# A convolution stage with its variance as one fp32 product, its casts on ScalarE and its low halves on VectorE

## The chip, the cores and the metric

The kernel runs on one core of one Trainium2 chip. The metric is the device time of one execution in microseconds (us). Five engines with queues of their own work side by side: TensorE (PE in the profile), VectorE (DVE), ScalarE (ACT), GpSimd (POOL) and SyncE (SP), which only issues DMAs here. They meet through semaphores: an instruction adds to one when it is done, another engine waits until it has reached a value.

## The reference, cut to what matters

The reference is a block of two layers on an image tensor of 16 x 64 x 56 x 56: a gated shift convolution and a mixture of experts, then a binary-weight convolution and a second mixture of experts. The stage in question computes the third and the fourth step of this:

```python
x = x + _L0_conv_ref(_ln_c(x), ...)
t = t + _L0_ffn_ref(_ln_t(t), ...)
x = x + _L1_conv_ref(_ln_c(x), L1_conv_weights, L1_conv_real_scaling_factor)   # this stage
t = t + _L1_ffn_ref(_ln_t(t), ...)     # its inner _ln_t(t) is made in this stage

def _ln_c(v, eps=1e-06):
    m = jnp.mean(v, axis=1, keepdims=True)
    s = jnp.var(v, axis=1, keepdims=True)
    return (v - m) / jnp.sqrt(s + eps)
```

`_L1_conv_ref` is a 3 x 3 convolution of 64 to 64 channels with the signs of the weights, padded by one pixel, times a factor for each output channel. `_ln_t` is the same normalisation over the channels with eps 1e-5.

## The kernel before, in words

The image tensor stays in SBUF as X, 56 tiles of 128 partitions (64 channels of two images) by 448 elements (8 rows of 56 pixels). Seven tiles make one pair of images. The stages before the one in question normalise, gate, shift, and run the first mixture of experts; those after it compute the routing of the second mixture (L1100 to L1203) and run it (L1208 to L1433). They read what this stage stores: XN4 (the normalised tile) and SD4 (its high and low half).

The stage runs from L871 to L1075. Each tile n is normalised (ln3), split into a high half in float32r and a low half (the rest), both written into padded images pad_hi and pad_lo; the convolution of tile n is 9 shifts times two halves, 18 products of 128 x 448 in float32r that accumulate in PSUM; X is updated with it; the new X is normalised again (ln4), split, and stored. ln3 runs three tiles ahead of the convolution (LEAD = 3), ln4 two tiles behind it.

One normalisation (class Norm, L120 to L224) is a chain through the engines:
- pe_centre (L158): PE multiplies the tile by the matrix CEN in fp32, which gives the tile minus its channel mean in PSUM. An fp32 product appears as two matmuls, each with a weight load.
- act_square: ACT squares it. With split set it does so twice, once rounded to float32r (sq_hi, L164) and once in fp32 (sq, L166). pool_square_lo (L173): POOL subtracts the one from the other.
- pe_var: with split set two float32r products with AVGR, of sq_hi (L182) and sq_lo (L183), into one PSUM tile; without it one fp32 product of sq with AVG (L187).
- act_r (L198) and act_rr (L204): ACT takes the reciprocal square root r and squares it.
- dve_newton: DVE computes q (L209) and g (L212), one Newton step. dve_scale (L219): DVE multiplies the centred tile by g.

ln3 and ln4 have two PSUM buffers for the centred tile and one for the variance, and one SBUF buffer for everything else (nx = 2, nv = 1, depth = 1). The other stages use Norm without split.

The order within a step n is written out by hand for each engine:
- PE: centre3(n+3), conv(n), var4(n-2), centre4(n-1), var3(n+3). The convolution waits until pad_lo of tile n+1 is written.
- ACT: squares of ln3(n+3), seed4(n-2) (r and rr), squares of ln4(n-1), seed3(n+3).
- DVE: norm3(n+2) (q, g, xn, and the cast into pad_hi, L1009), X(n) (L1028), norm4(n-2) (q, g, xn with a sum, and the cast into hi, L1017).
- POOL: low squares of ln3(n+3) (L173), lo3(n+2) (pad_lo, L1051), low squares of ln4(n-1), lo4(n-2) (lo, L1056).
- SP: stores of XN4 and of the two halves for tile n (L916, L919, L921).

The first 14 steps and the last 14 are unrolled, the 28 between run as two passes of a hardware loop with tile numbers in registers. The order of PE ahead of the first convolution is centre3(0), centre3(1), var3(0), centre3(2), var3(1), var3(2); POOL makes every low half there as well.

Of the kernel before, what the change touches and what calls it, by code (L numbers as in the profile page):

```python
# [16 lines left out]
F32 = mybir.dt.float32  # L17
F32R = mybir.dt.float32r
# [5 lines left out]
P = 128  # L24
# [22 lines left out]
def build(nc, A, out):  # L47
# [178 lines left out]
    with top:  # L226
# [644 lines left out]
        with ExitStack() as ctx:  # L871
# [3 lines left out]
            AVGR = sbuf(ctx, "average_r", [P, P], F32R)  # L875
# [11 lines left out]
            average_ready = sem(ctx, "p5_average")  # L887
# [9 lines left out]
            def every_step(engine, step):  # L897


                for i in units(engine, NP // 2 - 1):  # L900
                    for m in range(V):
                        step(V * i + m, m)
                for m in range(V):
                    step(NT - V + m, m)

            with nc.Block() as block:
                @block.sync
                def _(sp):
                    sp.dma_start(cwraw[:], A["conv_w"]).then_inc(consts, 16)
                    for a in range(2):  # L910
                        sp.dma_start(sf[C * a:C * a + C, :], A["factor"]).then_inc(consts, 16)

                    def store(n, m):

                        sp.wait_ge(ln4.normed, n + 1)
                        sp.dma_start(XN4[bass.ds(n, 1)].rearrange("o p w -> (o p) w"), xn4[:, m % 2])\  # L916
                            .then_inc(stored[m % 2], 16)
                        sp.wait_ge(hi_done, n + 1)
                        sp.dma_start(split_rows(SD4, n, 0), hi[:, m % 2].bitcast(F32)).then_inc(stored[m % 2], 16)  # L919
                        sp.wait_ge(lo_done, n + 1)  # L920
                        sp.dma_start(split_rows(SD4, n, 1), lo[:, m % 2].bitcast(F32)).then_inc(stored[m % 2], 16)  # L921

                    every_step(sp, store)
                    for b in range(2):
                        sp.wait_ge(stored[b], 48 * NT // 2)

                @block.tensor
                def _(pe):
                    pe.wait_ge(average_ready, 1)

                    def conv(n, m):
                        pair, k = divmod(m, KT)
                        pe.wait_ge(pad_lo_done, n + 1 + min(1, KT - 1 - k))
                        wait(pe, x3_done, n - 1)
                        o = rows(cps[:, m % 2, 0:TW])
# [7 lines left out]
                    def centre4(n, m):  # L943
                        pe.wait_ge(x3_done, n + 1)
                        ln4.pe_centre(pe, n, m, tile(X, n))

                    def step(n, m):
                        if exists(n + LEAD):
                            ln3.pe_centre(pe, n + LEAD, m + LEAD, tile(X, n + LEAD))
                        conv(n, m)  # L950
                        if exists(n - 2):
                            ln4.pe_var(pe, n - 2, m)
                        if exists(n - 1):
                            centre4(n - 1, m + 1)
                        if exists(n + LEAD):
                            ln3.pe_var(pe, n + LEAD, m + LEAD)

                    for k in range(LEAD):
                        ln3.pe_centre(pe, k, k, tile(X, k))
                        if k >= 1:  # L960
                            ln3.pe_var(pe, k - 1, k - 1)
                    ln3.pe_var(pe, LEAD - 1, LEAD - 1)
                    pe.wait_ge(signed, 1)
                    pe.wait_ge(zeroed, 8)
                    every_step(pe, step)
                    ln4.pe_var(pe, NT - 2, 0)
                    centre4(NT - 1, 1)
                    ln4.pe_var(pe, NT - 1, 1)

                @block.scalar  # L970
                def _(act):
                    act.activation(AVGR[:], AVG[:], ACT.Copy).then_inc(average_ready, 1)

                    def step(n, m):
                        if exists(n + LEAD):
                            ln3.act_square(act, n + LEAD, m + LEAD)
                        if exists(n - 2):
                            ln4.act_seed(act, n - 2, m, 1)
                        if exists(n - 1):
                            ln4.act_square(act, n - 1, m + 1)  # L980
                        if exists(n + LEAD):
                            ln3.act_seed(act, n + LEAD, m + LEAD, 0)

                    for k in range(LEAD):
                        ln3.act_square(act, k, k)
                        if k >= 1:
                            ln3.act_seed(act, k - 1, k - 1, 0)
                    ln3.act_seed(act, LEAD - 1, LEAD - 1, 0)
                    act.wait_ge(consts, 48)
                    act.activation(cw[:], cwraw[:], ACT.Sign).then_inc(signed, 1)  # L990
                    every_step(act, step)
                    ln4.act_seed(act, NT - 2, 0, 1)
                    ln4.act_square(act, NT - 1, 1)
                    ln4.act_seed(act, NT - 1, 1, 1)

                @block.vector
                def _(dve):
                    for border in borders(pad_hi):
                        dve.memset(border, 0.0).then_inc(zeroed, 1)

                    def norm3(n, m):

                        pair, k = divmod(m, KT)
                        wait(dve, pad_lo_done, n - 1)
                        ln3.dve_norm(dve, n, m, EPS_C, xn3[:, m % 2])
                        dve.wait_ge(ln3.normed, n + 1)
                        if k == 0:
                            wait(dve, conv_done, n - KT)
                        dve.tensor_copy(pad_hi[:, pair, ROWS * k + 1:ROWS * k + 1 + ROWS, 1:WW + 1], rows(xn3[:, m % 2]))\  # L1009
                            .then_inc(pad_hi_done, 1)  # L1010

                    def norm4(n, m):

                        wait(dve, stored[m % 2], past_stores(n, m))
                        ln4.dve_norm(dve, n, m, EPS_T, xn4[:, m % 2], accum=MSUM[:, bass.ds(n, 1)])
                        dve.wait_ge(ln4.normed, n + 1)
                        dve.tensor_copy(hi[:, m % 2], xn4[:, m % 2]).then_inc(hi_done, 1)  # L1017

                    def past_stores(n, m):

                        return 24 * (n - m % 2)

                    def step(n, m):
                        if exists(n - 1) and exists(n + LEAD - 1):
                            norm3(n + LEAD - 1, (m + LEAD - 1) % V)
                        dve.wait_ge(conv_done, n + 1)
                        x = tile(X, n)
                        dve.scalar_tensor_tensor(out=x, in0=cps[:, m % 2, 0:TW], scalar=sf[:, 0:1], in1=x,  # L1028
                                                 op0=ALU.mult, op1=ALU.add).then_inc(x3_done, 1)
                        if exists(n - 2):  # L1030
                            norm4(n - 2, m)

                    for k in range(LEAD):
                        norm3(k, k)
                    dve.wait_ge(consts, 48)
                    every_step(dve, step)
                    norm4(NT - 2, 0)
                    norm4(NT - 1, 1)

                @block.gpsimd  # L1040
                def _(pool):
                    for border in borders(pad_lo):
                        pool.memset(border, 0.0).then_inc(zeroed, 1)  # L1043

                    def lo3(n, m):
                        pair, k = divmod(m, KT)
                        inside = (slice(None), pair, slice(ROWS * k + 1, ROWS * k + 1 + ROWS), slice(1, WW + 1))
                        pool.wait_ge(pad_hi_done, n + 1)
                        if k == 0:
                            wait(pool, conv_done, n - KT)  # L1050
                        pool.tensor_tensor(pad_lo[inside], rows(xn3[:, m % 2]), pad_hi[inside].bitcast(F32), ALU.subtract)\  # L1051
                            .then_inc(pad_lo_done, 1)

                    def lo4(n, m):
                        pool.wait_ge(hi_done, n + 1)
                        pool.tensor_tensor(lo[:, m % 2], xn4[:, m % 2], hi[:, m % 2].bitcast(F32), ALU.subtract)\  # L1056
                            .then_inc(lo_done, 1)

                    def step(n, m):
                        if exists(n + LEAD):  # L1060
                            ln3.pool_square_lo(pool, n + LEAD, m + LEAD)
                        if exists(n - 1) and exists(n + LEAD - 1):
                            lo3(n + LEAD - 1, (m + LEAD - 1) % V)
# [441 lines left out]
```

## Time and profile before

| | us |
|---|---|
| median of 3 runs | 2896.38 |
| lowest and highest of the 3 | 2887.58 and 2897.5 |
| the profiled execution | 2888.95 |
| its span in the trace | 2887.0 |
| from the first product of the stage to its last GpSimd instruction | 2082.0 to 2469.0 |
| mean granted clock of PE over the span | 0.964 of full |
| PE busy over the span | 2641.3 (91%) |
| DVE busy over the span | 1493.1 (52%) |
| ACT busy over the span | 1582.3 (55%) |
| POOL busy over the span | 509.4 (18%) |

The profiled execution lies 7.4 us under the median: two of the three runs stand at 2896 to 2898 and one at 2888. Busy time over the span mixes eight stages. In what follows the time between the starts of two instructions is called their pitch. It differs from the duration that a row gives: a DVE or ACT instruction that depends on the one before starts a little after its end, an independent one up to 0.1 us before its end, and matmuls overlap further.

### The profile page before, as it was taken

The numbers are of one execution on the slowest core, as the hardware profiler recorded it, in microseconds if no ns is written. First come the engines' busy times: TensorE is split into PE (matmuls) and PEld (weight loads), VectorE is DVE, ScalarE is ACT, GpSimd is POOL, SyncE is SP. The second block draws the span as 40 slices with busy tenths as digits, with TensorE's granted clock in tenths as the row PEclk, the third lists the DMA queues.
The fourth block names the chain that finished last, engine by engine and source line by source line (L and its number), as shares of the span: only waits on it lengthen the run. The fifth ranks groups of instructions, "written<-read, shape, count | busy, mean of one in ns | idle before, by whom it ended". The sixth has DMA issues, their size and how long they took to land. (4 is left out here: it accounts for less than half of the span.)

```text
span 2887.0 us, 42401 instructions
## 1 busy us (share of the span) xinstructions
PE 2641.3 (91%) x12188; PEld 1488.0 (52%) x12188; DVE 1493.1 (52%) x2823; ACT 1582.3 (55%) x2305; POOL 509.4 (18%) x408
## 2 busy tenths in 40 slices
PE   8976786999999999999999999999889999298897
PEld 5642444555555555555555555555467777133343
DVE  6632888344444444444444444443369998245545
ACT  5630565555555555555555555555556665167666
POOL 3320775000000000000000000000068887100000
PEclk9988898999999999999999999999989999599999
DMA  4467676434243333424333342433113232475552
GB/s 133 131 144 161 176 201 179 107 76 96 64 97 75 86 87 74 96 64 97 77 83 90 72 96 65 96 78 83 41 58 115 106 115 106 116 181 150 163 158 81
DMA packets 168940, 308.47 MB, mean 107 GB/s; under 512 B 50626, under 2 KB 161058, under 8 KB 161570
## 3 DMA queue, kind: packets, MB, share of 16 engines
q1 hardware_dynamic: 168866, 307.60, 41.7%
q8 instruction: 32, 0.52, 0.1%
q14 instruction: 42, 0.34, 0.0%
HBM read 210.12 MB, written 97.39 MB: 107 GB/s over the span
## 5 line engine op out<-in xcount | busy, mean ns | idle before, releaser
L781 ACT ACTIVATE hidden<-hidden_psum,b 128x896 f32<-128x896 f32 x896 | 853.9, 1004 | 706.3 <-PE hidden_psum L730 706.3
L847 DVE SCALAR_TENSOR_TENSOR weighted<-y_psum,b,w_bc 128x448 f32<-128x448 f32 x448 | 306.4, 684 | 923.6 <-PE y_psum L744 909.8
L744 PE MATMUL y_psum<-hidden,w 128*64 128x448 f32 x3584 | 773.2, 552 | 2.1 <-DVE weighted L847 2.1
L729 PE MATMUL hidden_psum<-tokens,w1hi 128*128 128x448 f32 x1792 | 705.9, 394 | 14.0 <-DMA ident<-in_ident 11.2
L730 PE MATMUL hidden_psum<-tokens,w1lo 128*128 128x448 f32 x1792 | 660.5, 369 | 0.0
L729 PEld LDWEIGHTS hidden_psum<-tokens,w1hi 128*128 128x128 f32 x1792 | 336.7, 188 | 332.9 <-ACT hidden L781 294.2
L744 PEld LDWEIGHTS y_psum<-hidden,w 128*64 128x64 f32 x3584 | 217.7, 136 | 350.4 <-issue 244.0
L730 PEld LDWEIGHTS hidden_psum<-tokens,w1lo 128*128 128x128 f32 x1792 | 338.0, 189 | 24.3
L198 ACT ACTIVATE ln_r<-ln_var,eps 128x448 f32<-128x448 f32 x280 | 177.4, 634 | 235.9 <-PE ln_var L183 135.3
L158 PE MATMUL ln_xc<-X,centre 128*128 (+1 forms) x448 | 226.1, 588 | 74.7 <-DVE X L608 55.8
L1043 POOL MEMSET pad_lo<- 128x116 f32 (+1 forms) x4 | 0.8, 266 | 1591.6 <-POOLq L665 1591.6
L855 DVE TENSOR_TENSOR X<-X,weighted 128x448 f32 (+1 forms) x448 | 278.1, 621 | 2.9
L212 DVE SCALAR_TENSOR_TENSOR ln_g<-ln_q,ln_r 128x448 f32<-128x448 f32 x280 | 234.7, 838 | 9.7
L209 DVE SCALAR_TENSOR_TENSOR ln_q<-ln_var,ln_rr 128x448 f32<-128x448 f32 x280 | 172.9, 617 | 97.4 <-ACT ln_rr L204 96.0
L939 PE MATMUL conv_psum<-pad_hi,conv_sign 128*128 128x448 f32 x504 | 197.7, 392 | 1.5 <-POOL pad_lo L1051 1.4
L939 PE MATMUL conv_psum<-pad_lo,conv_sign 128*128 128x448 f32 x504 | 188.5, 374 | 0.0
L187 PE MATMUL ln_var<-ln_sq,average 128*128 128x448 f32 x336 | 163.2, 572 | 17.7 <-DVE ln_q L209 17.4
L1378 ACT ACTIVATE hidden<-hidden_psum,b1sel 128x448 f32<-128x448 f32 x224 | 130.3, 630 | 76.0 <-PE hidden_psum L1325 75.5
L166 ACT ACTIVATE ln_sq<-ln_xc 128x448 f32<-128x448 f32 x224 | 120.2, 537 | 93.9 <-PE ln_xc L158 93.8
L173 POOL TENSOR_TENSOR ln_sq_lo<-ln_sq,ln_sq_hi 128x448 fp32r<-128x448 f32 x112 | 160.9, 1437 | 45.1 <-ACT ln_sq L166 45.1
L204 ACT ACTIVATE ln_rr<-ln_r 128x448 f32<-128x448 f32 x280 | 161.7, 578 | 8.9
L219 DVE SCALAR_TENSOR_TENSOR xn<-ln_xc,ln_g 128x448 f32<-128x448 f32 x224 | 139.9, 625 | 40.0 <-DMA scr_xlr<-xn 20.1
(128 smaller groups left out, 2442.5 us busy)
## 6 DMA issues: line engine op xcount, KB each, us to landing
w_bc<-scr_wtok SPq DMA_DIRECT2D x112, 896.0 KB, 10.6
tokens<-scr_split SPq DMA_DIRECT2D x224, 224.0 KB, 3.7
scr_split<-hi SPq DMA_DIRECT2D x112, 224.0 KB, 2.0
scr_split<-lo SPq DMA_DIRECT2D x112, 224.0 KB, 1.9
scr_xn<-xn SPq DMA_DIRECT2D x56, 224.0 KB, 2.0
tokens_plus_y<-scr_xn SPq DMA_DIRECT2D x56, 224.0 KB, 2.8
out<-out_tile SPq DMA_DIRECT2D x56, 224.0 KB, 2.0
X<-in_x SPq DMA_DIRECT2D x6, 1792.0 KB, 7.6
```

What stands on the lines that cost most here:

```text
L158: pe.matmul(self.xc[:, b, 0:TW], CEN[:], x, start=True, stop=True).then_inc(self.centred, 1)
L187: pe.matmul(self.var[:, self.at(m, self.nv), 0:TW], AVG[:], self.sq[:, self.at(m, self.depth)], start=True, stop=True).then_inc(self.var_r ...
L198: act.activation(self.r[:, b], self.var[:, self.at(m, self.nv), 0:TW], ACT.Abs_reciprocal_sqrt, bias=EPS[:, eps_col:eps_col + 1]).then_inc ...
L209: dve.scalar_tensor_tensor(out=self.q[:, b], in0=self.var[:, self.at(m, self.nv), 0:TW], scalar=eps, in1=self.rr[:, b], op0=ALU.add, op1=A ...
L212: dve.scalar_tensor_tensor(out=self.g[:, b], in0=self.q[:, b], scalar=-3.0, in1=self.r[:, b], op0=ALU.add, op1=ALU.mult).then_inc(self.g_d ...
L729: pe.matmul(o, w1hi[:, s * P:(s + 1) * P], S[:, b, a, :], start=True, stop=False)
L730: mm = pe.matmul(o, w1lo[:, s * P:(s + 1) * P], S[:, b, a, :], start=False, stop=True)
L744: mm = pe.matmul(yp[C * a:C * a + C, e % 2, 0:TW], w2[:, e, c, :], hs[:, s % (2 * CH0), a, :], start=(c == 0), stop=(c == CH0 - 1))
L781: act.activation(hs[:, k % (2 * CH0)], hp[:, k % 2, :, 0:TW], ACT.Gelu, bias=b1[:, e, c:c + 1])\
L847: dve.scalar_tensor_tensor(out=pr[:, e % 2], in0=yp[:, e % 2, 0:TW], scalar=b2[:, e:e + 1], in1=WB[:, b, e, :], op0=ALU.add, op1=ALU.mult) ...
L855: dve.tensor_tensor(x, x, pr[:, e % 2], ALU.add).then_inc(summed, 1)
L939: mm = pe.matmul(o, cw[:, t9, :], src[:, pair, ROWS * k + dy:ROWS * k + dy + ROWS, dx:dx + WW], start=(t9 == 0 and part == 0), stop=(t9 == ...
```

## The change

In the convolution stage alone:
- ln3 and ln4 are made without split: one square on ACT (L166), one fp32 product on PE (L187) instead of two float32r ones, no low squares. AVGR goes, and the wait for it.
- The casts into pad_hi and hi move from DVE to ACT (high3, high4, ACT Copy).
- The subtractions into pad_lo and lo move from POOL to DVE (low3, low4). POOL keeps only the zeroing of pad_lo's borders.
- The steps are all unrolled, without registers.
- Orders: PE runs centre3(n+3) behind conv(n) instead of ahead of it, and centre3, var3 tile by tile at the start. ACT runs high3(n+2), square3(n+3), seed4(n-2), square4(n-1), seed3(n+3), high4(n-2). DVE runs norm3(n+2), low3(n+2), X(n), norm4(n-2), low4(n-2).

```diff
-            ln3 = Norm(ctx, "ln3", 2, 1, depth=1, split=AVGR)
-            ln4 = Norm(ctx, "ln4", 2, 1, depth=1, split=AVGR)
+            ln3 = Norm(ctx, "ln3", 2, 1, depth=1)
+            ln4 = Norm(ctx, "ln4", 2, 1, depth=1)
...
                 @block.tensor
...
+                    for n in range(LEAD):
+                        centre3(n)
+                        ln3.pe_var(pe, n, n)
                     pe.wait_ge(signed, 1)
                     pe.wait_ge(zeroed, 8)
...
+                    for n in range(NT):
+                        conv(n)
+                        if n + LEAD < NT:
+                            centre3(n + LEAD)
+                        if n >= 2:
+                            ln4.pe_var(pe, n - 2, n - 2)
+                        if n >= 1:
+                            centre4(n - 1)
+                        if n + LEAD < NT:
+                            ln3.pe_var(pe, n + LEAD, n + LEAD)
...
                 @block.scalar
...
+                    def high3(n):
+                        act.wait_ge(ln3.normed, n + 1)
+                        if n % KT == 0 and n >= V:
+                            act.wait_ge(conv_done, n - KT)
+                        act.activation(inside(pad_hi, n), rows(xn3[:, n % 2]), ACT.Copy).then_inc(pad_hi_done, 1)
+
+                    def high4(n):
+                        act.wait_ge(ln4.normed, n + 1)
+                        if n >= 2:
+                            act.wait_ge(stored[n % 2], 48 * (n // 2))
+                        act.activation(hi[:, n % 2], xn4[:, n % 2], ACT.Copy).then_inc(hi_done, 1)
+
+                    for n in range(LEAD):
+                        ln3.act_square(act, n, n)
+                        ln3.act_seed(act, n, n, 0)
+                        if n < LEAD - 1:
+                            high3(n)
                     act.wait_ge(consts, 48)
                     act.activation(cw[:], cwraw[:], ACT.Sign).then_inc(signed, 1)
...
+                    for n in range(NT + 2):
+                        if n + LEAD - 1 < NT:
+                            high3(n + LEAD - 1)
+                        if n + LEAD < NT:
+                            ln3.act_square(act, n + LEAD, n + LEAD)
+                        if 2 <= n:
+                            ln4.act_seed(act, n - 2, n - 2, 1)
+                        if 1 <= n <= NT:
+                            ln4.act_square(act, n - 1, n - 1)
+                        if n + LEAD < NT:
+                            ln3.act_seed(act, n + LEAD, n + LEAD, 0)
+                        if 2 <= n:
+                            high4(n - 2)
...
                 @block.vector
...
+                    def low3(n):
+                        dve.wait_ge(pad_hi_done, n + 1)
+                        if n % KT == 0 and n >= V:
+                            dve.wait_ge(conv_done, n - KT)
+                        dve.tensor_tensor(inside(pad_lo, n), rows(xn3[:, n % 2]), inside(pad_hi, n).bitcast(F32), ALU.subtract)\
+                            .then_inc(pad_lo_done, 1)
...
+                    def low4(n):
+                        dve.wait_ge(hi_done, n + 1)
+                        dve.tensor_tensor(lo[:, n % 2], xn4[:, n % 2], hi[:, n % 2].bitcast(F32), ALU.subtract)\
+                            .then_inc(lo_done, 1)
```

## Rows read from the trace of the kernel before

**Rows 1.** Windows of the stage: busy of PE, PEld, DVE, ACT, POOL; clock; DMA.

```profile
2113.00:2454.00 341.00, 339.54 (x1414) 260.10 (x1413) 310.95 (x532) 214.69 (x424) 268.69 (x212) 1.00 0.29 106
...
2082.00:2107.00 25.00, 7.67 (x15) 3.21 (x15) 6.89 (x15) 8.79 (x14) 5.80 (x7) 0.60 0.08 24
```

**Rows 2.** Timeline of one step, PE: start, duration, instruction, idle before it.

```profile
2251.47 0.37 PE L939 MATMUL conv_psum<-pad_lo,conv_sign 128*128 128x448 f32 x1
...
2254.82 0.37 PE L939 MATMUL conv_psum<-pad_lo,conv_sign 128*128 128x448 f32 x1
...
2255.43 0.92 PE L158 MATMUL ln_xc<-X,centre 128*128 x2
...
2257.30 0.19 PEld L939 LDWEIGHTS conv_psum<-pad_hi,conv_sign 128*128 128x128 f32 x1 [0.51 <-POOL pad_lo L1051]
```

**Rows 3.** Timeline of the last stage: weight loads of unsplit variance products.

```profile
2728.47 0.19 PEld L187 LDWEIGHTS ln_var<-ln_sq,average 128*128 128x128 f32 x1 [0.19 <-issue]
...
2729.22 0.19 PEld L187 LDWEIGHTS ln_var<-ln_sq,average 128*128 128x128 f32 x1 [0.19 <-issue]
```

**Rows 4.** Timeline of the stage: one step of DVE, and the rr that releases it.

```profile
2256.98 0.62 DVE L209 SCALAR_TENSOR_TENSOR ln_q<-ln_var,ln_rr 128x448 f32<-128x448 f32 x1 [0.29 <-ACT ln_rr L204]
...
2260.10 1.14 DVE L212 SCALAR_TENSOR_TENSOR ln_g<-ln_q,ln_r 128x448 f32<-128x448 f32 x1
...
2262.45 0.58 ACT L204 ACTIVATE ln_rr<-ln_r 128x448 f32<-128x448 f32 x1
...
2263.13 0.62 DVE L209 SCALAR_TENSOR_TENSOR ln_q<-ln_var,ln_rr 128x448 f32<-128x448 f32 x1
```

**Rows 5.** Timeline of the second normalisation's stage: DVE to ACT to POOL.

```profile
487.54 0.62 DVE L219 SCALAR_TENSOR_TENSOR xn<-ln_xc,ln_g 128x448 f32<-128x448 f32 x1
...
488.20 0.58 ACT L581 ACTIVATE hi<-xn 128x448 fp32r<-128x448 f32 x1 [2.48 <-DVE xn L219]
...
488.85 1.13 POOL L543 TENSOR_TENSOR lo<-xn,hi 128x448 fp32r<-128x448 f32 x1 [1.93 <-ACT hi L581]
```

**Rows 6.** The same stage: ACT.

```profile
305.56 0.53 ACT L166 ACTIVATE ln_sq<-ln_xc 128x448 f32<-128x448 f32 x1
305.98 0.63 ACT L198 ACTIVATE ln_r<-ln_var,eps 128x448 f32<-128x448 f32 x1
306.64 0.58 ACT L204 ACTIVATE ln_rr<-ln_r 128x448 f32<-128x448 f32 x1
...
310.41 0.56 ACT L581 ACTIVATE hi<-xn 128x448 fp32r<-128x448 f32 x1
310.88 0.52 ACT L166 ACTIVATE ln_sq<-ln_xc 128x448 f32<-128x448 f32 x1
```

**Rows 7.** The same stage: DVE, a two-input subtraction's like.

```profile
305.98 0.62 DVE L608 TENSOR_TENSOR X<-X,shifted 128x448 f32<-128x448 f32 x1
306.52 0.62 DVE L209 SCALAR_TENSOR_TENSOR ln_q<-ln_var,ln_rr 128x448 f32<-128x448 f32 x1
307.17 0.62 DVE L212 SCALAR_TENSOR_TENSOR ln_g<-ln_q,ln_r 128x448 f32<-128x448 f32 x1
307.83 0.62 DVE L219 SCALAR_TENSOR_TENSOR xn<-ln_xc,ln_g 128x448 f32<-128x448 f32 x1
```

**Rows 8.** Timeline, the 56 updates of X: tiles 0, 34 and 55.

```profile
2112.99 0.68 DVE L1028 SCALAR_TENSOR_TENSOR X<-conv_psum,factor,X 128x448 f32<-128x448 f32 x1 [5.76 <-PE conv_psum L939]
...
2325.09 0.67 DVE L1028 SCALAR_TENSOR_TENSOR X<-conv_psum,factor,X 128x448 f32 x1
...
2454.33 0.68 DVE L1028 SCALAR_TENSOR_TENSOR X<-conv_psum,factor,X 128x448 f32<-128x448 f32 x1 [0.61 <-PE conv_psum L939]
```

**Rows 9.** Timeline: a table load, the first convolution product, the last of POOL.

```profile
2087.14 1.28 ACT L198 ACT_TABLE_LOAD   x1
...
2106.84 1.25 PE L939 MATMUL conv_psum<-pad_hi,conv_sign 128*128 128x448 f32 x1
...
2467.89 1.13 POOL L1056 TENSOR_TENSOR lo<-xn,hi 128x448 fp32r<-128x448 f32 x1 [3.54 <-DVE hi L1017]
```

More of the change, by code:

```diff
@@ L874, in build @@
             sf = sbuf(ctx, "factor", [P, 1])
-            AVGR = sbuf(ctx, "average_r", [P, P], F32R)
             pad_hi = sbuf(ctx, "pad_hi", [P, 2, HH + 2, PADW], F32R)
@@ L895, in borders, with inside @@
                 return p[:, :, 0, :], p[:, :, HH + 1, :], p[:, :, 1:HH + 1, 0], p[:, :, 1:HH + 1, WW + 1]
[L897 to L904, printed above, removed]
+            def inside(pad, n):
+                pair, k = divmod(n % V, KT)
+                return pad[:, pair, ROWS * k + 1:ROWS * k + 1 + ROWS, 1:WW + 1]
             with nc.Block() as block:
@@ L911, in _, with conv @@
                         sp.dma_start(sf[C * a:C * a + C, :], A["factor"]).then_inc(consts, 16)
-                    def store(n, m):
+                    for n in range(NT):
+                        b = n % 2
                         sp.wait_ge(ln4.normed, n + 1)
-                        sp.dma_start(XN4[bass.ds(n, 1)].rearrange("o p w -> (o p) w"), xn4[:, m % 2])\
-                            .then_inc(stored[m % 2], 16)
+                        sp.dma_start(XN4[n], xn4[:, b]).then_inc(stored[b], 16)
                         sp.wait_ge(hi_done, n + 1)
-                        sp.dma_start(split_rows(SD4, n, 0), hi[:, m % 2].bitcast(F32)).then_inc(stored[m % 2], 16)
+                        sp.dma_start(SD4[n, 0], hi[:, b].bitcast(F32)).then_inc(stored[b], 16)
                         sp.wait_ge(lo_done, n + 1)
-                        sp.dma_start(split_rows(SD4, n, 1), lo[:, m % 2].bitcast(F32)).then_inc(stored[m % 2], 16)
-                    every_step(sp, store)
+                        sp.dma_start(SD4[n, 1], lo[:, b].bitcast(F32)).then_inc(stored[b], 16)
                     for b in range(2):
                         sp.wait_ge(stored[b], 48 * NT // 2)
+                @block.gpsimd
+                def _(pool):
+                    for border in borders(pad_lo):
+                        pool.memset(border, 0.0).then_inc(zeroed, 1)
                 @block.tensor
                 def _(pe):
-                    pe.wait_ge(average_ready, 1)
-                    def conv(n, m):
-                        pair, k = divmod(m, KT)
+                    def conv(n):
+                        pair, k = divmod(n % V, KT)
                         pe.wait_ge(pad_lo_done, n + 1 + min(1, KT - 1 - k))
-                        wait(pe, x3_done, n - 1)
-                        o = rows(cps[:, m % 2, 0:TW])
+                        if n >= 2:
+                            pe.wait_ge(x3_done, n - 1)
+                        o = rows(cps[:, n % 2, 0:TW])
                         for t9 in range(9):
@@ L941, in conv, with centre3, centre4 @@
                         mm.then_inc(conv_done, 1)
-                    def centre4(n, m):
+                    def centre3(n):
+                        ln3.pe_centre(pe, n, n, X[:, n])
+                    def centre4(n):
                         pe.wait_ge(x3_done, n + 1)
[L945 to L962, printed above, removed]
+                        ln4.pe_centre(pe, n, n, X[:, n])
+                    for n in range(LEAD):
+                        centre3(n)
+                        ln3.pe_var(pe, n, n)
                     pe.wait_ge(signed, 1)
                     pe.wait_ge(zeroed, 8)
-                    every_step(pe, step)
@@ L966, in _ @@
-                    ln4.pe_var(pe, NT - 2, 0)
-                    centre4(NT - 1, 1)
-                    ln4.pe_var(pe, NT - 1, 1)
+                    for n in range(NT):
+                        conv(n)
[7 more added lines that the diff above has]
+                            ln3.pe_var(pe, n + LEAD, n + LEAD)
@@ L970, in _ @@
+                    ln4.pe_var(pe, NT - 2, NT - 2)
+                    centre4(NT - 1)
+                    ln4.pe_var(pe, NT - 1, NT - 1)
                 @block.scalar
                 def _(act):
[L972 to L988, printed above, removed]
+                    def high3(n):
[3 more added lines that the diff above has]
+                        act.activation(inside(pad_hi, n), rows(xn3[:, n % 2]), ACT.Copy).then_inc(pad_hi_done, 1)
@@ new lines, in high4 @@
+                    def high4(n):
+                        act.wait_ge(ln4.normed, n + 1)
+                        if n >= 2:
+                            act.wait_ge(stored[n % 2], 48 * (n // 2))
[5 more added lines that the diff above has]
+                            high3(n)
@@ L996, in _, with norm3 @@
                 @block.vector
                 def _(dve):
+                    def norm3(n):
+                        if n >= 2:
+                            dve.wait_ge(pad_lo_done, n - 1)
+                        ln3.dve_norm(dve, n, n, EPS_C, xn3[:, n % 2])
+                    def low3(n):
[4 more added lines that the diff above has]
+                            .then_inc(pad_lo_done, 1)
@@ L998, in _, with norm4 @@
+                    def norm4(n):
+                        if n >= 2:
+                            dve.wait_ge(stored[n % 2], 48 * (n // 2))
+                        ln4.dve_norm(dve, n, n, EPS_T, xn4[:, n % 2], accum=MSUM[:, n:n + 1])
+                    def low4(n):
+                        dve.wait_ge(hi_done, n + 1)
+                        dve.tensor_tensor(lo[:, n % 2], xn4[:, n % 2], hi[:, n % 2].bitcast(F32), ALU.subtract)\
+                            .then_inc(lo_done, 1)
                     for border in borders(pad_hi):
@@ L999, in _ @@
                         dve.memset(border, 0.0).then_inc(zeroed, 1)
[L1001 to L1031, printed above, removed]
@@ L1033, in _ @@
-                    for k in range(LEAD):
-                        norm3(k, k)
-                    dve.wait_ge(consts, 48)
[L1036 to L1063, printed above, removed]
-                        if exists(n - 1):
-                            ln4.pool_square_lo(pool, n - 1, m + 1)
-                        if exists(n - 2):
-                            lo4(n - 2, m)
-                    for k in range(LEAD):
-                        ln3.pool_square_lo(pool, k, k)
-                        lo3(k, k)
-                    every_step(pool, step)
-                    ln4.pool_square_lo(pool, NT - 1, 1)
-                    lo4(NT - 2, 0)
-                    lo4(NT - 1, 1)
@@ new lines, in _ @@
+                    for n in range(LEAD - 1):
+                        norm3(n)
+                        low3(n)
+                    dve.wait_ge(consts, 48)
+                    for n in range(NT + 2):
+                        if n + LEAD - 1 < NT:
+                            norm3(n + LEAD - 1)
+                        if n + LEAD - 1 < NT:
+                            low3(n + LEAD - 1)
+                        if n < NT:
+                            dve.wait_ge(conv_done, n + 1)
+                            dve.scalar_tensor_tensor(out=X[:, n], in0=cps[:, n % 2, 0:TW], scalar=sf[:, 0:1], in1=X[:, n],
+                                                     op0=ALU.mult, op1=ALU.add).then_inc(x3_done, 1)
+                        if n >= 2:
+                            norm4(n - 2)
+                            low4(n - 2)
```

5 lines of the change are left out of this document (removed).

## The prediction

> **What bounds the kernel now.** I read the windows first, then the timeline of one step, then the rows of X(n). Only one stage changes, so only its share of the span matters. In its steady part PE is busy 339.5 of 341 us at full clock and DVE 311 of 341, ACT 215 and POOL 269 [rows 1]. PE's busy time counts overlapping matmuls, so pitches have to confirm it. The 56 updates of X run from 2112.99 to 2454.33: 55 steps of 6.206 us [rows 8].
>
> PE in a step: 16 pitches of convolution products take 3.35 us, 0.209 each, so 18 take 3.77. From the last of them to the centring behind the variance pair are 0.61, so the pair costs 0.40 [rows 2]. An fp32 product is two matmuls: three weight loads of the unsplit variance lie 0.375 apart (2728.47, one left out between, 2729.22), so one product costs 0.75 [rows 3]. A step has 3.77 + 2 x 0.40 + 2 x 0.75 = 6.07 us of array work in 6.206. PE then waits for pad_lo from POOL for a moment: its weight loader stood 0.51 us, of which the array feels about 0.1, since the centring still drains [rows 2].
>
> DVE in the same step goes from q3 to the next q3 in 6.15 us, nearly without a gap, and one of its two g instructions takes 1.14 instead of 0.62 us [rows 4, 7]. So both engines are full today: work taken from one gains nothing alone, and work or a wait added to either lengthens the step.
>
> **The change part by part, PE.** Each of the two variance pairs becomes one fp32 product: 0.40 to 0.75. The step's array work is 3.77 + 4 x 0.75 = 6.77 us. Nothing hides it: 0.56 over the step of today. This is a floor for the new step.
>
> **DVE and ACT.** DVE loses two casts, gains two subtractions of two SBUF operands, and is rid of POOL's company. But each subtraction now waits for a cast that ACT can only begin when DVE's xn is done: DVE stands still for a round trip twice a step. DVE to ACT: from the start of xn to the start of the copy 0.66 us; from there to the start of the waiting subtraction 0.65 [rows 5] (the waiter there is POOL; DVE behind ACT's rr waits 0.68 from rr's start, whose duration is the same 0.58 [rows 4], so the price for each trip lies between 0.65 and 0.68 and I take 0.65).
>
> ACT is in order too. high3(n+2) stands ahead of square3 and seed4, so DVE's q4 can't start until ACT went through all of them. Pitches on ACT: copy 0.47, square 0.42, r 0.66 [rows 6], and rr to q 0.68 [rows 4]. On DVE: q 0.65, g 0.66, and subtraction to an independent q 0.54 (the row is an addition of two SBUF tiles in the same shape, 0.62 us long) [rows 7].
>
> I follow one step from q3 at 0: xn3 at 1.31; high3 on ACT at 1.97; square3 at 2.44; r4 at 2.86; rr4 at 3.52; q4 at 4.20. DVE's own path to q4 is shorter: low3 at 1.97 + 0.65 = 2.62, X at 3.16, free at about 3.87, so q4 is held 0.3 us by ACT. Then xn4 at 5.51; high4 on ACT at 6.17 (ACT is free from about 5.7: square4 at 4.0, r3 at 4.4, rr3 at 5.1); low4 at 6.82; the next q3 at 7.36. Step 7.36 us.
>
> Does PE hold any of this back? Its 6.77 leave 0.59 of slack, which falls in front of var3(n+3): that needs square3, done at about 3.0. conv(n+1) then runs from 3.8 to 7.5, centre3 to 8.3, var4 to 9.05. In the next step's count these are 0.9 and 1.7, ahead of 2.44 and 2.86. low3(n+2) is written at 3.25, ahead of conv(n+1). centre3 behind the convolution instead of ahead of it costs nothing by this. The stores of a buffer have two steps to land. So the loop through DVE and ACT sets the step, at +1.15 us over 6.206.
>
> **Start of the stage.** Before, POOL stands in each of the three first chains, and the first convolution starts at 2106.84 [rows 9]. After: with the first centring at 2081.7 and the square at 2082.75, r waits for a table load of 1.28 us [rows 9], and xn3(0) ends at 2087.9. Each further tile is one chain of copy, square, variance, r, rr, q, g, xn without overlap: about 0.55 + 0.55 + 1.9 + 0.67 + 0.68 + 1.93 = 6.3 us, where 1.9 is the fp32 product at half clock (the granted clock is 0.60 over this stretch [rows 1], and PE idles more now). xn3(1) ends at 2094.3; square, variance, r, rr of tile 2 and the signs take 5.3: the first convolution at 2099.6, 7.3 us earlier than today, its end as much earlier.
>
> **Steps and tail.** X(0) at 2105.7. The first three steps are irregular (PE late, then a lag of 1.05 us once): X(3) at 2126.8. Then 50 steps of 7.36: X(53) at 2494.8. The last two steps lack ln3 and take 4.2 and 3.8: X(55) at 2502.8. From X(0) to X(55) these are 397.1 us against 341.3 [rows 8]: +55.8. Behind X(55) three rounds of q, g, xn, copy and subtraction (3.3 each) take 10.2 us to the end of the last subtraction, against 14.7 today (2454.33 to 2467.89 + 1.13 [rows 8, 9]): -4.5.
>
> Sum: -7.3 + 55.8 - 4.5 = +44.0 us.
>
> **Unrolling.** Costed at nothing. The loop holds tiles 14 to 41. The first 34 steps, over half of them in it, take 6.24 us each, the last 21, a third of them in it, 6.15 [rows 8]: what an unrolled step may save is of the order of 0.1. With DVE waiting, a branch would be hidden as well. Bounds: 0.1 us x 28 = 3 us gained, 3 us lost to code loading.
>
> **POOL and the shared port.** The row shows a g of 1.14 us where POOL computes beside it, against 0.62 elsewhere [rows 4, 7]: 0.52 a step that comes back. It is in my sum already, as every DVE pitch is of undisturbed rows. The Trainium skill (SBUF - State Buffer, "Who interferes with whom") says that VectorE's instructions with two SBUF inputs contend for a port pair with GpSimd instructions that read SBUF; the trace agrees by that row. By that rule alone, with a VectorE that bounds the stage, leaving GpSimd out would make the stage faster: that is the third rival.
>
> **Against the times.** On the profiled execution's 2888.95 the sum gives 2933. The runs before fall into a group near 2897 and one near 2888; on the median the same sum gives 2940. I forecast 2937, between.
>
> **Rivals.** (1) PE alone sets the step, at 6.77. It would be so if the two round trips were hidden. Against it: one buffer depth and the order written out leave DVE nothing else to do between xn and low. 50 x 0.59 = 30 less: +14, about 2907, at the edge of what can be told from no change.
>
> (2) The clock. PE is full-clocked at 99.6% busy; after, it works 6.77 of 7.36 us (92%) with a short stop in each step. If the granted clock fell to 0.9 in the mean, its work would be 7.5 us and the step with it: +7 us more. At 0.8 it would be 8.5: +56 more, about 2993. Against it: over the whole span, PE is 91% busy and the mean clock 0.96.
>
> (3) The other side: the stage gets faster, because DVE is what binds. DVE's instructions without any wait are 5.7 us a step (2 x 1.31 + 2 x 0.66 + 2 x 0.54 + 0.7), 0.4 less than today's 6.15. With the fp32 product at no more than the pair's 0.40, and the copies done before DVE looks for them, the step would be 6.07: -7.5 over 55 steps, with start and tail -19, 2872 on my middle. It decides from a step under 6.42 us on, where start and tail outweigh the rest. Against it: 0.75 for the product, in every unsplit row of the other stages.
>
> (4) The round trips cost more than priced, or PE and DVE hold each other up in turn: steps of 7.6 to 7.8, +12 to +22 more, up to 2959.
>
> **How the numbers follow.** Chances: the forecast 0.70, PE alone 0.12, the clock 0.04, faster 0.03, dearer trips 0.11. The forecast's own range is 2925 to 2949: 0.03 us for each round trip and 0.05 for each of the other unknown pitches make the step 7.3 to 7.5 (-3 to +7), unrolling 3 each way, and the two levels of the runs 4 each way. It holds 0.70, so the range takes in what lies next: down to the PE-bound case at 2907, up to most of case 4 at 2957. A measurement of this kernel tells about 0.5% (14 us) from no change: under 2882 faster, to 2911 the same. Faster 0.03; the same 0.11 (nearly all of the first rival); slower 0.86.
>
> **What would show it.** X(n) 7.3 to 7.5 us apart; the first convolution product near 2099.6; the longest waits of the stage those of DVE's two subtractions for ACT's copies, about 0.6 us before each, and of q4 for rr of some 0.3; no g over 0.7 us; PE standing before var3 for the square (about 0.6 a step) and the stage's clock still 1.00. If PE has no gap and steps are 6.8, the first rival holds. If q4 has no wait, ACT's order is not what I think. Stages before and after should not move; if they do, the prediction is wrong for a reason that I don't have.

## The result, and the profile after

| | before | changed |
|---|---|---|
| median of 4 runs each, us | 2894.8 | 2936.1 |
| lowest and highest | 2887.6 to 2897.5 | 2935.3 to 2939.1 |
| profiled execution | 2888.95 | 2939.14 |
| its span | 2887.0 | 2937.1 |

The changed kernel is slower by some 1.5%: the ratio is 1.0149, 95% interval 1.0128 to 1.0169, 41.3 us between the medians. Between the two profiled executions it is 50.2, because the one of before lies 5.9 under its median and the one of after 3.0 above.

The stage alone, from its first centring to the end of its last subtraction, took 387.0 us and takes 435.2: +48.2. The stages ahead of it differ by 2.2 us, those behind by 0.3. The first lies within what the start of the stage moves between kernels that differ only inside it: from 2081.9 us to 2087.2 in the eleven traces.

The updates of X in the changed kernel, from a timeline of VectorE (start, duration, instruction, idle before it; L1035 is L1028 of before). They answer [rows 8].

```profile
2107.53 0.68 DVE L1035 SCALAR_TENSOR_TENSOR X<-conv_psum,factor,X 128x448 f32<-128x448 f32 x1 [3.78 <-PE conv_psum L933]
...
2253.95 0.68 DVE L1035 SCALAR_TENSOR_TENSOR X<-conv_psum,factor,X 128x448 f32<-128x448 f32 x1
...
2261.31 0.68 DVE L1035 SCALAR_TENSOR_TENSOR X<-conv_psum,factor,X 128x448 f32<-128x448 f32 x1
...
2506.51 0.68 DVE L1035 SCALAR_TENSOR_TENSOR X<-conv_psum,factor,X 128x448 f32<-128x448 f32 x1
```

A step is 7.35 to 7.36 us in all but a few of the 55, against 6.206, which is the mean over all 55 of before, the irregular three at either end among them; the 49 between take 6.27. In what follows q3, xn3 are instructions of ln3, q4, xn4 of ln4, high is ScalarE's copy and low VectorE's subtraction. One step in the changed kernel, the whole loop through VectorE and ScalarE, from its timeline:

```profile
2250.83 0.62 DVE L209 SCALAR_TENSOR_TENSOR ln_q<-ln_var,ln_rr 128x448 f32<-128x448 f32 x1
...
2252.14 0.63 DVE L219 SCALAR_TENSOR_TENSOR xn<-ln_xc,ln_g 128x448 f32<-128x448 f32 x1
...
2252.80 0.58 ACT L969 ACTIVATE pad_hi<-xn 128x448 fp32r<-128x448 f32 x1 [2.55 <-DVE xn L219]
2253.28 0.53 ACT L166 ACTIVATE ln_sq<-ln_xc 128x448 f32<-128x448 f32 x1
2253.41 0.63 DVE L1009 TENSOR_TENSOR pad_lo<-xn,pad_hi 128x448 fp32r<-128x448 f32 x1 [0.64 <-ACT pad_hi L969]
2253.71 0.63 ACT L198 ACTIVATE ln_r<-ln_var,eps 128x448 f32<-128x448 f32 x1
...
2253.86 1.02 PE L187 MATMUL ln_var<-ln_sq,average 128*128 128x448 f32 x2 [0.29 <-ACT ln_sq L166]
...
2254.37 0.58 ACT L204 ACTIVATE ln_rr<-ln_r 128x448 f32<-128x448 f32 x1
...
2255.05 0.62 DVE L209 SCALAR_TENSOR_TENSOR ln_q<-ln_var,ln_rr 128x448 f32<-128x448 f32 x1 [0.41 <-ACT ln_rr L204]
...
2256.36 0.62 DVE L219 SCALAR_TENSOR_TENSOR xn<-ln_xc,ln_g 128x448 f32<-128x448 f32 x1
...
2257.03 0.58 ACT L975 ACTIVATE hi<-xn 128x448 fp32r<-128x448 f32 x1 [0.52 <-DVE xn L219]
...
2257.64 0.62 DVE L1019 TENSOR_TENSOR lo<-xn,hi 128x448 fp32r<-128x448 f32 x1 [0.65 <-ACT hi L975]
2258.18 0.62 DVE L209 SCALAR_TENSOR_TENSOR ln_q<-ln_var,ln_rr 128x448 f32<-128x448 f32 x1
```

Counted from q3 at 2250.83: xn3 1.31, high3 1.97, square 2.45, r4 2.88, rr4 3.54, q4 4.22, xn4 5.53, high4 6.20, low4 6.81, next q3 7.35. VectorE stands still three times, 0.64 and 0.65 for the copies and 0.41 for rr. None of ScalarE's squares waits for a centring, so PE's new order, which no run takes alone, isn't on this loop.

The waits of the stage's steady part, 2150 to 2450 us (engine, line, what it waited for: us in total, times, longest):

```profile
ACT pad_hi L969 <- DVE xn L219: 104.3, 41, 2.5
PEld ln_var L187 <- ACT ln_sq L166: 42.1, 41, 1.4
DVE lo L1019 <- ACT hi L975: 26.5, 41, 0.6
DVE pad_lo L1009 <- ACT pad_hi L969: 26.4, 41, 0.6
ACT hi L975 <- DVE xn L219: 21.6, 41, 0.9
DVE ln_q L209 <- ACT ln_rr L204: 17.3, 41, 0.8
...
PE ln_var L187 <- ACT ln_sq L166: 12.5, 41, 0.7
```

The top line is ScalarE waiting for work, which costs nothing. VectorE's three add up to 70.2 us in 41 steps, 1.71 each. PE stands too (0.3 a step by the last line, 1.0 by its weight loader's): neither engine is full, in a stage where PE was busy 339.5 of 341 us before and VectorE went through its step nearly without a gap [rows 1, 4]. The window of the steady part, columns as in [rows 1]:

```profile
2150.00:2400.00 250.00, 239.96 (x885) 164.10 (x884) 187.48 (x340) 143.70 (x273) 0.00 (x0) 1.00 0.26 94
```

### The profile page after: what moved, and what is told of

The parts are those of the page before. It is cut to its first block and busy times, and to the rows that moved or that the text cites. A ratio compares the mean times of both kernels' runs of the same rounds, so it can differ in the third digit from the quotient of the medians.

```text
span 2937.1 us, 41684 instructions
## 1 busy us (share of the span) xinstructions
PE 2690.2 (92%) x12188; PEld 1493.8 (51%) x12188; DVE 1477.6 (50%) x2823; ACT 1593.8 (54%) x2304; POOL 227.0 (8%) x184
## 5 line engine op out<-in xcount | busy, mean ns | idle before, releaser
L187 PE MATMUL ln_var<-ln_sq,average 128*128 128x448 f32 x560 | 275.9, 577 | 42.5 <-ACT ln_sq L166 21.9
L158 PE MATMUL ln_xc<-X,centre 128*128 128x448 f32 (+1 forms) x448 | 226.0, 588 | 62.9 <-DVE X L608 52.3
L212 DVE SCALAR_TENSOR_TENSOR ln_g<-ln_q,ln_r 128x448 f32<-128x448 f32 x280 | 208.4, 744 | 9.6
L933 PE MATMUL conv_psum<-pad_hi,conv_sign 128*128 128x448 f32 x504 | 207.9, 412 | 3.7 <-ACT conv_sign L983 2.4
L187 PEld LDWEIGHTS ln_var<-ln_sq,average 128*128 128x128 f32 x560 | 98.2, 194 | 154.9 <-ACT ln_sq L166 95.1
L166 ACT ACTIVATE ln_sq<-ln_xc 128x448 f32<-128x448 f32 x224 | 119.4, 533 | 102.7 <-PE ln_xc L158 102.6
L158 PEld LDWEIGHTS ln_xc<-X,centre 128*128 128x128 f32 x448 | 80.1, 197 | 139.3 <-issue 120.9
```

The costliest lines, as they stand in the source:

```text
L158: pe.matmul(self.xc[:, b, 0:TW], CEN[:], x, start=True, stop=True).then_inc(self.centred, 1)
L187: pe.matmul(self.var[:, self.at(m, self.nv), 0:TW], AVG[:], self.sq[:, self.at(m, self.depth)], start=True, stop=True).then_inc(self.var_r ...
L212: dve.scalar_tensor_tensor(out=self.g[:, b], in0=self.q[:, b], scalar=-3.0, in1=self.r[:, b], op0=ALU.add, op1=ALU.mult).then_inc(self.g_d ...
L933: mm = pe.matmul(o, cw[:, t9, :], src[:, pair, ROWS * k + dy:ROWS * k + dy + ROWS, dx:dx + WW], start=(t9 == 0 and part == 0), stop=(t9 == ...
```

## The experiments

Theory A is the prediction's: in each step VectorE and ScalarE hand work to and fro on one chain, which sets the step at 7.36 us. Its main rival B: the fp32 product makes TensorE's work longer, and that is what the step shows. "Stage" is measured as above; a median's difference holds the noise of whole runs, some 3 us.

| kernel | median | ratio to before, 95% interval | median step | stage |
|---|---|---|---|---|
| before | 2894.8 | | 6.21 | 387.0 |
| changed | 2936.1 | 1.0128 to 1.0169 | 7.35 | 435.2 |
| variance alone | 2907.5 | 1.0030 to 1.0064 | 6.79 | 406.0 |
| moves alone | 2970.0 | 1.0255 to 1.0296 | 7.79 | 465.7 |
| round trips hidden | 2907.8 | 1.0029 to 1.0062 | 6.79 | 405.7 |
| one rounded product | 2934.3 | 1.0127 to 1.0160 | 7.35 | 432.9 |
| one more copy | 2962.5 | 1.0225 to 1.0259 | 7.82 | 460.0 |
| one more copy, trips hidden | 2908.0 | 1.0034 to 1.0068 | 6.79 | 406.9 |
| seed ahead of the square | 2975.1 | 1.0265 to 1.0300 | 8.07 | 471.7 |
| before, unrolled | 2890.8 | 0.9985 to 1.0005 | 6.22 | 387.5 |
| best | 2847.7 | 0.9829 to 0.9861 | 5.69 | 345.7 |

Each ratio is to runs of the kernel before on the same chip, whose medians were 2891.8 to 2894.8. Differences to the changed kernel are between medians from different chips.

**Take the waits away.** VectorE is given other work while ScalarE copies:

```diff
                             norm3(n + LEAD - 1)
+                        if n >= 3:
+                            low4(n - 3)
...
                             norm4(n - 2)
-                            low4(n - 2)
```

> The changed kernel, with one order altered: VectorE runs low4(n-3) between xn3(n+2) and low3(n+2) instead of low4(n-2) right behind xn4(n-2), so that both casts on ScalarE run while VectorE has other work. Theory A (the loop through VectorE and ScalarE with two round trips sets the step of 7.36 us): VectorE's loop falls to about 6.2, TensorE's array work of 6.77 becomes the bound, steps of 6.8, 28 to 32 us less than the changed kernel: about 2906. Rival B (the dearer fp32 product on TensorE is what lengthened the step, the round trips lie beside it): steps stay at 7.3 to 7.4, 0 to 5 us less.

The step is 6.79 and the median 28.3 us under the changed kernel. Rival B is out for the part between 6.79 and 7.36. The window shows the other bound:

```profile
2150.00:2400.00 250.00, 250.00 (x958) 180.48 (x957) 199.55 (x369) 163.62 (x295) 0.00 (x0) 1.00 0.28 103
```

PE without a gap, at the 6.77 that its array work was counted to.

**Take the dearer product away.** Norm's square is written as float32r, and the variance is one float32r product of it:

```diff
-            self.sq = sbuf(ctx, tag + "_sq", [P, depth, TW])
+            self.sq = sbuf(ctx, tag + "_sq", [P, depth, TW], F32R if rounded else F32)
...
-            pe.matmul(self.var[...], AVG[:], self.sq[...],
+            pe.matmul(self.var[...], (self.rounded or AVG)[:], self.sq[...],
```

> The changed kernel, but the squares of ln3 and ln4 are rounded to float32r and the variance is one float32r product of them, 0.20 us instead of 0.75 (this leaves out the squares' low halves). TensorE's array work falls from 6.77 to 5.67 us a step. Theory A: steps stay at 7.36, as TensorE had slack anyway; only the three chains at the start, the lag in the third step and the tail gain, 3 to 7 us together: about 2931. Rival B: steps fall by 0.6 to 1.1, 30 to 60 us less than the changed kernel.

The step doesn't move, 7.35, though PE had 1.1 us a step less to do; the stage is 2.3 us shorter, from its start (1.1) and its steps and tail, less than the 3 to 7 expected. The waits of 2150 to 2400 show where PE's spare time goes, 1.4 us a step:

```profile
PEld ln_var L188 <- ACT ln_sq L167: 70.8, 34, 2.1
PE ln_var L188 <- ACT ln_sq L167: 46.3, 34, 1.4
```

With the experiment before it this settles which loop holds the changed kernel: shortening PE's work by 1.1 gives nothing, hiding VectorE's waits gives 0.57.

**Make the chain longer, in both.** A copy of xn3 into a spare tile, ahead of the one into pad_hi:

```diff
+                        act.activation(spare[:], xn3[:, n % 2], ACT.Copy)
                         act.activation(inside(pad_hi, n), ..., ACT.Copy).then_inc(pad_hi_done, 1)
```

> The changed kernel, with one more copy of xn3 on ScalarE, into a spare tile, ahead of the copy into pad_hi. Theory A (the copy lies on the loop through VectorE and ScalarE that sets the step): the copy's pitch of 0.47 us goes in full into each step, 7.83 us, over 54 steps 25 us more than the changed kernel: about 2961. Rival B (TensorE sets the step): no change, since ScalarE is busy 58% of the stage and TensorE has all it needs.

> The same extra copy, in the kernel whose round trips are hidden (low4 between xn3 and low3, 2907.8 us). There TensorE sets the step with 6.79, and the loop through VectorE and ScalarE needs about 6.2. Theory A: 6.2 + 0.47 = 6.67 stays under 6.79, so 0 to 3 us more, about 2909. If the copy costs 20 us here too, the loop still sets the step in the kernel with hidden trips, and TensorE's bound is not what held it at 6.79.

7.82 a step and 26.4 us more in the one, 6.79 and 0.2 us more in the other. The same instruction costs its full pitch (0.47) where it lies on the chain and nothing where TensorE binds.

**ScalarE's order.** The prediction had q4 held 0.3 us behind square3. Moving the seed up looks like the cure:

```diff
+                        if 2 <= n:
+                            ln4.act_seed(act, n - 2, n - 2, 1)
                         if n + LEAD < NT:
                             ln3.act_square(act, n + LEAD, n + LEAD)
-                        if 2 <= n:
-                            ln4.act_seed(act, n - 2, n - 2, 1)
```

> The changed kernel, with ScalarE running seed4(n-2) ahead of the square of ln3(n+3) (high3, seed4, square3, ...). Theory A followed through all engines: now TensorE's var3(n+3) waits for a square that stands behind seed4, which itself waits for var4: conv 3.77 + centre 0.75 + var4 0.75 + 0.17 + r 0.66 + rr 0.48 + square 0.54 + 0.05 + var3 0.75 = 7.92 us a step, 26 to 30 us more than the changed kernel: about 2964. Rival D (the only thing that counts on ScalarE is that q4 is held by 0.3 us behind the square): steps of 7.0 to 7.1, 12 to 18 us less.

It costs 39 us. The rival is out and the direction was right, the size was not: 8.07 a step instead of 7.92. Its timeline:

```profile
2300.00 1.02 PE L187 MATMUL ln_var<-ln_sq,average 128*128 128x448 f32 x2 [1.01 <-ACT ln_sq L166]
...
2304.66 0.92 PE L158 MATMUL ln_xc<-X,centre 128*128 128x448 f32 x2
...
2305.42 0.91 PE L187 MATMUL ln_var<-ln_sq,average 128*128 128x448 f32 x2
...
2306.37 0.63 ACT L198 ACTIVATE ln_r<-ln_var,eps 128x448 f32<-128x448 f32 x1 [0.47 <-PE ln_var L187]
...
2307.04 0.58 ACT L204 ACTIVATE ln_rr<-ln_r 128x448 f32<-128x448 f32 x1
2307.52 0.96 ACT L166 ACTIVATE ln_sq<-ln_xc 128x448 f32<-128x448 f32 x2
...
2308.10 0.30 PEld L187 LDWEIGHTS ln_var<-ln_sq,average 128*128 128x128 f32 x2 [1.73 <-ACT ln_sq L166]
```

From one var3 (2300.00) over the convolution to centre3 are 4.66 us, where 0.75 + 3.77 = 4.52 were counted: the product that restarts PE behind a wait takes 1.02 us, the next 0.91. That restart is most of the 0.15 that was missing. The chain is the one that was written down: var4, r, rr, square, var3.

**The parts alone.** The kernel before with the unsplit variance and nothing else (no low squares on GpSimd), and the changed kernel with the split variance put back:

```diff
-            ln3 = Norm(ctx, "ln3", 2, 1, depth=1, split=AVGR)
+            ln3 = Norm(ctx, "ln3", 2, 1, depth=1)
...
-                            ln3.pool_square_lo(pool, n + LEAD, m + LEAD)
```

> The kernel before with the variance alone changed: one fp32 product of unsplit squares, no low squares on GpSimd; casts stay on VectorE, low halves on GpSimd, the loop stays. Theory A: VectorE's own loop is 6.1 or less, TensorE binds with 6.77 of array work, steps of 6.8 to 6.85: +33 us over 55 steps, the start about 3 us shorter without GpSimd in its chains: +27 to +33 against the kernel before. Rival E (the kernel before was bound by VectorE and GpSimd, not by TensorE, and gains by the rest from the low squares): within 10 us of the kernel before.

> The changed kernel with the variance as in the kernel before: split squares, low squares on GpSimd, two float32r products. Only the casts (on ScalarE), the low halves (on VectorE), the orders and the unrolling are changed. Theory A: the same loop with one more square on ScalarE (0.43 us) between high3 and seed4 gives 7.8 us a step; GpSimd's low squares now lie beside g again and may lengthen it by up to 0.5: 7.8 to 8.3, over 53 steps 23 to 50 more than the changed kernel, 2960 to 2986, although TensorE's array work is back at 6.07 us. Rival B (TensorE's dearer product is what costs): back near the kernel before, under 2910.

The variance alone gives 6.79 a step, as counted, and 14.2 us in the medians, 18.9 in the stage. That is less than expected: the steps come to +27.3 us and not 33, since the first and the last few are shorter than the rest; the start is 5.6 us shorter, not 3; and the tail, which I had not counted, 2.7. The moves alone give 7.79, at the low end of the expectation, and are the dearest of the three: +78.7 in the stage. So the parts don't add up: +18.9 and +78.7 alone, +48.2 together. Two loops run through the stage and the longer one counts; the unsplit variance takes one square off the chain that the moves create, and its pitch of 0.43 is the whole of 7.79 less 7.36. Its own price on PE vanishes below that chain. GpSimd's low squares are not on it: PE stands 1.4 us a step for them (45.2 in 32 times, 2150 to 2400), as it has that slack, and g was not lengthened either, which the expectation allowed for (0.633 us in the mean).

**Unrolling.**

```diff
-                for i in units(engine, NP // 2 - 1):
-                    for m in range(V):
-                        step(V * i + m, m)
-                for m in range(V):
-                    step(NT - V + m, m)
+                for n in range(NT):
+                    step(n, n % V)
```

> The kernel before with its stage fully unrolled and nothing else changed. Prediction: VectorE and TensorE fill the step, branches lie beside them, so within 3 us of the kernel before either way. Rival F (the loop's branches and register work cost on the path): 6 us or more less. If code loading costs, 3 us or more above.

No difference: the stage 387.5 against 387.0, the medians 1.7 apart within the interval.

**A version that beats both.** From the same recurrence, with the rounded product of the second experiment (not shown again) and orders chosen so that neither engine should wait:

```diff
-                        conv(n)
                         if n + LEAD < NT:
                             centre3(n + LEAD)
+                        conv(n)
...
+                        if n + LEAD < NT:
+                            ln3.act_square(act, n + LEAD, n + LEAD)
                         if n + LEAD - 1 < NT:
                             high3(n + LEAD - 1)
-                        if n + LEAD < NT:
-                            ln3.act_square(act, n + LEAD, n + LEAD)
...
+                        if n >= 3:
+                            low4(n - 3)
                         if n < NT:
                             dve.wait_ge(conv_done, n + 1)
                             dve.scalar_tensor_tensor(out=X[:, n], ...)
+                        if n + LEAD - 1 < NT:
+                            low3(n + LEAD - 1)
```

> A version meant to beat both: squares rounded to float32r and one float32r product for the variance (the squares' low halves are left out), centre3 ahead of the convolution as in the kernel before; ScalarE runs square3 ahead of high3, then seed4; VectorE runs norm3(n+2), low4(n-3), X(n), low3(n+2), norm4(n-2). Theory A: TensorE has 5.67 us a step, VectorE 5.7, and by the same recurrence q4 starts 3.78 after q3 and the next q3 at 5.64 to 5.75. Steps of 5.7 to 5.9: 16 to 27 us less than the kernel before over the steps, another 8 to 11 from start and tail: 2855 to 2869. If the steps stay above 6.1, the recurrence misses a wait.

2847.7 us: 44.7 under the runs of before beside it (ratio 0.9845, interval 0.9829 to 0.9861), 88 under the changed kernel. Steps of 5.69, where PE's 5.67 was counted: from 2150 to 2400 PE is busy 250.00 us of 250. VectorE still waits 0.23 a step for rr (10.0 in 44 times), so its own work is under 5.5 and not the 5.7 that was counted. It beat its expectation by 7 us: start and tail gave 11.7, just over the 8 to 11 expected, and the steps 29.7 instead of 16 to 27 (311.65 from X(0) to X(55)). It rounds the squares and leaves their low halves out, as only one_rounded does beside it, so part of its gain is bought with precision of the variance; no run takes its orders without that.

## Why the prediction was right

It forecast 2937 and 2936.1 was measured, but part of that closeness is luck of the base: the sum of +44.0 us was 4.2 too small against the stage's 48.2, and the two profiled executions lie apart from their medians by 8.9 in sum. By its steps:

- **The loop, 7.36 us.** Measured 7.35 to 7.36, each of its ten stations within 0.03 us. trips_hidden, one_rounded and the two extra copies show that it is this loop.
- **PE, 6.77 us.** Right, seen bare where the trips are hidden and where the variance alone is changed (6.79 both). That it had slack in the changed kernel was right as well.
- **Round trips.** From copy to subtraction 0.61, priced at 0.65; from xn to copy 0.66 and 0.67, priced at 0.66. VectorE stands 0.41 before q4, forecast 0.3: the X ahead of it was free sooner (3.80 and not 3.87 in the step's count). PE's stop before var3, forecast at about 0.6 a step, is 0.3 by its own rows and 1.0 by its weight loader's.
- **Start, -7.3 us.** Measured -7.7: from the first centring to X(0) 23.3 us against 31.0, and to the first convolution product (2101.51) 17.3 against 24.8. One round of the start takes 6.02 us (q of tile 0 at 2089.05, of tile 1 at 2095.07) instead of 6.3, since only the first of the three variance products took the full 1.9 us; the others took 1.67 and 1.02. The granted clock of 2084 to 2102.5 was 0.72, against 0.60 in [rows 1], though PE was expected to idle more.
- **Steps, +55.8.** Measured 398.98 us against 341.34, +57.6. The lag of about 1 us in the third step is there (8.34). The last two steps took 4.22 and 5.27, not 4.2 and 3.8: 1.5 of the missing 1.8; one step of 7.72 is the rest.
- **Tail, -4.5.** This is the term that was mis-sized: 12.9 us and not 10.2, so -1.8. First, q of tile 53 starts 2.10 us behind X(55), where the sum left it 0.3: it waits 1.41 for rr, because PE makes that tile's variance (2506.31) only behind the last products of the convolution. The last step holds the same wait of 1.41, which is why it takes 5.27. Second, a round takes 3.79 (q of tile 53, 54 and 55 at 2508.61, 2512.40, 2516.20) and not 3.3:

```profile
2508.61 0.63 DVE L209 SCALAR_TENSOR_TENSOR ln_q<-ln_var,ln_rr 128x448 f32<-128x448 f32 x1 [1.41 <-ACT ln_rr L204]
...
2510.59 0.58 ACT L975 ACTIVATE hi<-xn 128x448 fp32r<-128x448 f32 x1 [1.66 <-DVE xn L219]
...
2511.08 0.62 ACT L198 ACTIVATE ln_r<-ln_var,eps 128x448 f32<-128x448 f32 x1
...
2511.72 0.58 ACT L204 ACTIVATE ln_rr<-ln_r 128x448 f32<-128x448 f32 x1
...
2512.40 0.62 DVE L209 SCALAR_TENSOR_TENSOR ln_q<-ln_var,ln_rr 128x448 f32<-128x448 f32 x1 [0.58 <-ACT ln_rr L204]
```

high4(n) stands ahead of seed4(n+1) on ScalarE, so r and rr of the next tile start only behind the copy, while the prediction let them run beside xn. It is the same effect that was counted in the steps and forgotten at the end.
- **Unrolling at nothing** and **the stage's clock at 1.00**: both as forecast; before_unrolled shows the first, the window above the second. The reading behind the first was wrong, though: the last 21 steps took 6.15 in the mean because the three last are short (5.92, 5.36, 4.92), not because fewer of them lie in the loop. Without these three it is 6.28, and the 28 steps from X(14) to X(42) take 6.27.
- **The g of 1.14 us comes back**: none over 0.7. The mean of 106 g is 625 ns, against 874 in the same part of the kernel before.

Of the rivals, the PE-bound one is what trips_hidden makes of the kernel, at 2907.8, the time that it was priced at. The other side (faster) had its condition, 0.75 for the product, against it. best meets both its conditions, a cheap product and copies done in time, and is faster, but with PE full: so it doesn't show that VectorE alone binds the kernel before. (That rival's price is 2 us off by its own terms: 19 under 2893 is 2874, not 2872.)

## What to carry to other kernels

Where an order is written out by hand and buffers are one deep, follow one step through all engines, with pitches and not durations, and look for every loop: the longest sets the step, and what is taken off or put on another one changes nothing (1.1 us of PE's work: none; one copy of 0.47: all of it or none). Moving work to an idle engine puts a round trip on the chain, here 0.65 us each time, unless the engine that waits is given something else in between, which here was a matter of one reordered line. Count the drain of the pipeline by the same recurrence as its steps, through every engine: here ScalarE's copy and PE's order both stood in it.

## What was not expected of the hardware

GpSimd and VectorE hinder each other in either direction, and in these rows the one that is under way first keeps its time. In the kernel before, g at 2260.10 meets a subtraction of GpSimd's that began 0.49 us ahead of it and takes 1.14 us instead of 0.62 [rows 4]. The other g of each step begins first there and keeps its 0.62, and it is GpSimd's subtraction that takes 1.39 to 1.40 instead of 1.13. The first line is that of the kernel before, the others show the second order in moves_alone:

```profile
2259.61 1.15 POOL L1056 TENSOR_TENSOR lo<-xn,hi 128x448 fp32r<-128x448 f32 x1 [0.33 <-DVE hi L1017]
...
2308.42 0.62 DVE L212 SCALAR_TENSOR_TENSOR ln_g<-ln_q,ln_r 128x448 f32<-128x448 f32 x1
...
2308.67 1.39 POOL L173 TENSOR_TENSOR ln_sq_lo<-ln_sq,ln_sq_hi 128x448 fp32r<-128x448 f32 x1 [0.87 <-ACT ln_sq L166]
```

One step of the changed kernel took 7.72 us: q4 began at 2402.49, 0.45 us behind the end of the rr that releases it instead of 0.10. The same step is longer by the same 0.35 in the kernels with hidden trips (7.14) and with one rounded product (7.70); before and before_unrolled don't show it. In moves_alone it is longer by 1.26 (9.05), and there the other 0.91 is explained: q4 is late by 0.35, so GpSimd's subtraction begins first for once (2425.47, g at 2425.57), and this g takes 1.54 us. No run here tells the cause of the 0.35.
